# Two FFN tiles shared by chunks 1 and 2 and three shared by chunks 3 and 2, as products of 512 columns

## What is computed

```python
x = x + tanh(g_xattn) * wkv(w, u, layernorm(x), ctx)      # a decaying scan over the 128 positions
n = layernorm(x)
h = fwht(n * SU_ug) / 64                                  # Hadamard transform, 256 wide
g, up = h @ W_gate.T * (Wscale_gate * 64), h @ W_up.T * (Wscale_up * 64)   # 256 -> 1024
h = fwht(silu(g) * up * SU_dp) / 64                       # 1024 wide
x = x + tanh(g_ffn) * (h @ W_down.T * (Wscale_dp * 64))   # 1024 -> 256
```

## Time and profile before

| | us |
|---|---|
| median of 3 runs | 110.94 |
| lowest, highest | 109.91, 111.43 |
| profiled execution, its own time | 110.77 |
| its span, first to last instruction | 109.0 |
| PE busy in it | 102.0 (94%) |
| DVE, ACT, POOL busy | 69.7, 68.1, 61.2 |

### The profile page before, as it was taken

The page is one execution under the profiler, slowest core; times in us unless marked ns, Lnnn a source line. Parts: engine busy times, 40 slices in busy tenths (PEclk is TensorE's granted clock), DMA queues, the critical chain, the costliest instruction groups (busy, mean ns, idle before and its releaser), DMA issues.

```text
span 109.0 us, 2031 instructions
## 1 busy us (share of the span) xinstructions
PE 102.0 (94%) x728; PEld 92.4 (85%) x728; DVE 69.7 (64%) x146; ACT 68.1 (63%) x153; POOL 61.2 (56%) x73
## 2 busy tenths in 40 slices
PE   6999999798999999978999999699999999999990
PEld 5787797477667999968999989699999999999980
DVE  0399987599999995798998259932277221134211
ACT  4099969889929899925337995555975532442400
POOL 7026995996995994149996246355207243234400
PEclk9999999999999999999999999999999999999998
DMA  1899999200000000000000000020000200000202
GB/s 63 269 359 384 387 415 403 111 3 6 0 0 0 0 6 0 0 0 3 0 0 6 0 0 0 0 102 0 0 0 3 96 6 0 0 3 0 96 6 96
DMA packets 2893, 7.70 MB, mean 71 GB/s; under 512 B 321, under 2 KB 706, under 8 KB 2754
## 3 DMA queue, kind: packets, MB, share of 16 engines
q1 hardware_dynamic: 2882, 7.56, 18.6%
HBM read 6.51 MB, written 1.05 MB: 69 GB/s over the span
## 4 chain that ended last, share of the span: by engine, by line
PE 59%; ACT 14%; DVE 14%; issue 9%; DVEq 0%; POOL 0%; ACTq 0%; POOLq 0%
PE UG L960 24%; PE VB L833 9%; PE OD L998 5%; PE VB L998 3%; PE FX L998 3%; PE KZ L998 3%; ACT L558 2%; PE FX L923 2%; ACT L561 2%; DVE DEN L720 2%; PE FX L877 2%; DVE SQ L664 2%; PE OD L890 2%; PE VB L890 2%; PE KZ L890 2%
## 5 line engine op out<-in xcount | busy, mean ns | idle before, releaser
L478 POOL TENSOR_TENSOR HL<-H,HH 128x256 fp32r<-128x256 f32 x32 | 26.0, 817 | 30.0 <-ACT HH L617 29.9
L810 DVE SCALAR_TENSOR_TENSOR H<-S,ALPHA,UG 128x256 f32<-128x256 f32 x32 | 15.0, 476 | 17.5 <-ACT S L626 17.4
L626 ACT ACTIVATE S<-UG,HI 128x256 f32<-128x256 f32 x32 | 14.8, 467 | 14.6 <-PE UG L960 14.6
L960 PE MATMUL UG<-FH,WTH 128*128 128x256 f32 x128 | 21.8, 293 | 0.8 <-DVE H L810 0.7
L617 ACT ACTIVATE HH<-H 128x256 fp32r<-128x256 f32 x32 | 13.2, 411 | 12.3 <-DVE H L810 12.2
L960 PE MATMUL UG<-FL,WTH 128*128 128x256 f32 x128 | 20.2, 280 | 0.5 <-DVE FL L781 0.5
L960 PE MATMUL UG<-FH,WTL 128*128 128x256 f32 x128 | 20.1, 279 | 0.0
L960 PEld LDWEIGHTS UG<-FH,WTH 128*128 128x128 f32 x128 | 17.6, 189 | 2.4 <-issue 1.2
L960 PEld LDWEIGHTS UG<-FL,WTH 128*128 128x128 f32 x128 | 17.2, 189 | 0.7 <-DVE FL L781 0.7
L960 PEld LDWEIGHTS UG<-FH,WTL 128*128 128x128 f32 x128 | 17.2, 188 | 0.0
L833 PE MATMUL VB<-ONES 128*128 128x256 f32 x32 | 9.9, 470 | 1.0 <-POOL ONES L432 1.0
(11 more groups left out here) (154 smaller groups left out, 220.7 us busy)
## 6 DMA issues: line engine op xcount, KB each, us to landing
WN<-in_weights SPq DMA_DIRECT2D x4, 512.0 KB, 9.9
DN<-in_w_down SPq DMA_DIRECT2D x1, 1024.0 KB, 7.0
out<-XT SPq DMA_DIRECT2D x3, 256.0 KB, 2.5
X<-in_x SPq DMA_DIRECT2D x2, 256.0 KB, 3.9
V<-in_ct SPq DMA_DIRECT2D x2, 256.0 KB, 8.0
XT<-in_xt SPq DMA_DIRECT2D x2, 256.0 KB, 9.9
X<-in_x SPq DMA_DIRECT2D x1, 512.0 KB, 9.9
V<-in_ct SPq DMA_DIRECT2D x1, 512.0 KB, 12.7
```

The lines of the kernel that those rows point to most:

```text
L478: pool.tensor_tensor(HL[:, q % JT, 0:n], ring(H, q), HH[:, q % JT, 0:n].bitcast(F32), ALU.subtract).then_inc(h_lo, 1)
L626: act.activation(ring(S, q), gate_part(q), ACT.Silu, scale=VT[:, V_SGATE + j:V_SGATE + j + 1]).then_inc(silu_ready, 1)
L810: dve.scalar_tensor_tensor(out=ring(H, q), in0=ring(S, q), scalar=ALPHA[:, j:j + 1], in1=up_part(q), op0=ALU.mult, op1=ALU.mult).then_inc( ...
L960: return pe.matmul(dst.rearrange("p (g n) -> p g n", n=GT), w[:, m, j, t, :], f[:, chunks, t, :], start=start, stop=stop, skip_group_check ...
```

## The change

- The order of slots is now a list `PASSES`, 27 slots in place of 32: chunk 0 with tiles 0 to 7, chunk 1 with tiles 0 to 5, chunks 1 and 2 together with tiles 6 and 7, chunk 2 with tiles 0 to 2, chunks 3 and 2 together with tiles 3 to 5, chunk 3 with tiles 6, 7, 0, 1, 2. A shared slot ("wide" below: 14, 15, 19, 20, 21) has the same 12 up products and 6 down products, of 512 columns. Its gate part and its up part fill a bank each, and ACT, DVE and POOL work on 512 columns in it.
- The totals: chunk 0 has the halves of OD; then KZ holds t = 0 and OD t = 1, chunks 1 and then 3 in the left half, chunk 2 in the right half. FX and VB hold none. Between chunks 1 and 3 DVE writes zeros into the left halves (`emptied`).
- The down products follow a table `DOWNS`. None stands behind slots 13, 24, 25 and 26; the last five slots' products are left for the end (`TAIL` = 4).
- The halves of the squares aren't added by POOL any more: `ones` of chunks 2 and 3 takes two products in place of one.
- Steps move: `ones` 2 from slot 12 to 10, `fwht` 3 from 17 to 16, `ones` 3 from 19 to the same slot 16; ACT's steps with them, with `f_hi` of chunks 2 and 3 now inside the `exp_block`, ahead of the second table load.

```diff
+PASSES = (((0,), range(JT)), ((1,), range(6)), ((1, 2), (6, 7)), ((2,), range(3)), ((3, 2), range(3, 6)), ((3,), (6, 7, 0, 1, 2)))
+ROWS = [(chunks, j) for chunks, js in PASSES for j in js]
+HOME = (3, 1, 2, 0)
...
 PE_STAGES
     9: [("fwht", 2)],
-    12: [("ones", 2)],
-    17: [("fwht", 3)],
-    19: [("ones", 3)],
+    10: [("ones", 2)],
+    16: [("fwht", 3), ("ones", 3)],
 ACT_STAGES
     9: [("square", 2)],
-    12: [("exp_block", (("rstd2", 2), ("recip", 3))), ("f_hi", 2)],
-    15: [("x_hi", 3)],
-    17: [("square", 3)],
-    19: [("exp_block", (("rstd2", 3),)), ("f_hi", 3)],
+    10: [("exp_block", (("rstd2", 2), ("recip", 3), ("f_hi", 2)))],
+    14: [("x_hi", 3)],
+    16: [("square", 3), ("exp_block", (("rstd2", 3), ("f_hi", 3)))],
 DVE_STAGES
     6: [("x_lo", 2), ("scan_a", 3)],
-    8: [("mix_den", 3), ("scan_av", 3)],
-    9: [("mix_num", 3)],
-    12: [("root", 2), ("f_scaled", 2), ("f_lo", 2), ("estimate", 3)],
+    9: [("mix_den", 3)],
+    10: [("root", 2), ("f_scaled", 2), ("f_lo", 2), ("scan_av", 3)],
+    12: [("out", 0), ("mix_num", 3), ("estimate", 3)],
     13: [("newton", 3), ("x1", 3)],
-    15: [("x_lo", 3)],
-    19: [("root", 3), ("f_scaled", 3), ("f_lo", 3)],
+    14: [("x_lo", 3)],
+    16: [("root", 3), ("f_scaled", 3), ("f_lo", 3)],
+    18: [("out", 1)],
+    23: [("out", 2)],
 POOL_STAGES
-    5: [("av", 3)],
-    6: [("x1_first", 0)],
-    8: [("sum", 2)],
-    11: [("error", 3)],
-    17: [("sum", 3)],
+    6: [("av", 3)],
+    9: [("x1_first", 0), ("error", 3)],
+DOWNS = {
+    6: [0], 7: [1], 8: [2], 9: [3], 10: [4], 11: [5], 12: [6, 7], 14: [8, 9], 15: [10, 11], 16: [12], 17: [13, 14], 18: [15], 19: [16, 17],
+    20: [18], 21: [19], 22: [20], 23: [21],
+}
+TAIL = 4
...
 out_of, DVE
+                if g == 1:
+                    dve.wait_ge(out_ready, CT * g + t + 1)
+                    dve.memset(total(LAST, t), 0.0).then_inc(emptied, 1)
...
 down, PE
+                    if first(q, 0) and t == 0:
+                        wait_shared(pe, "m_lo", M_FULL[3])
+                    elif first(q, 1) and t == 0:
+                        pe.wait_ge(a_ready, NG)
+                    elif first(q, 1):
+                        pe.wait_ge(out_ready, CT)
+                    elif final(q - 1, 1):
+                        pe.wait_ge(emptied, t + 1)
...
 behind the last up, PE
+            left = range(max(r for rs in DOWNS.values() for r in rs) + 1, SLOTS)
+            for n, r in enumerate(left[:-1]):
+                pe.wait_ge(h_lo, r + 1)
...
+                down_part(r, 0)
+            for n, r in enumerate(left[:TAIL]):
...
+                down_part(r, 1)
             pe.wait_ge(h_lo, SLOTS)
             down_part(SLOTS - 1, 0)
+            for r in left[TAIL:]:
+                down_part(r, 1)
```

More of the change, by code:

```diff
@@ L33 @@
 NBANKS = 4
-LAG = 6
-TAIL = 3
 WHOLE = ()
@@ L111, in places, with first, final @@
     return [g for n, g in stages(table) if n == name]
-def group(q):
-    return q // JT
 def width(q):
-    return GT * len(GROUPS[group(q)])
+    return GT * len(ROWS[q][0])
+def first(q, g):
+    return g in ROWS[q][0] and not any(g in ROWS[r][0] for r in range(q))
+def final(q, g):
+    return g in ROWS[q][0] and not any(g in ROWS[r][0] for r in range(q + 1, SLOTS))
+UNITS = []
+for q in range(SLOTS):
+    n = width(q) // GT
+    u = UNITS[-1][-1] + 1 if UNITS else 0
+    u += u % n
+    UNITS.append(range(u, u + n))
 FILLS = []
@@ L138 @@
 M_FULL = places(PE_STAGES, "m")
+SUMMED = places(POOL_STAGES, "sum")
 SHARED = ("norm1", "av", "error", "w_lo", "m_lo", "fly", "x_lo")
@@ L235, in build @@
         e_ready, f_scaled, f_hi, f_lo = (sem(n) for n in ("e_ready", "f_scaled", "f_hi", "f_lo"))
-        silu_ready, h_ready, h_hi, h_lo, down_full, out_ready = (sem(n) for n in (
-            "silu_ready", "h_ready", "h_hi", "h_lo", "down_full", "out_ready"))
+        silu_ready, h_ready, h_hi, h_lo, down_full, out_ready, emptied = (sem(n) for n in (
+            "silu_ready", "h_ready", "h_hi", "h_lo", "down_full", "out_ready", "emptied"))
         def arrival(g):
@@ L256, in ring @@
         def ring(tile, q):
-            n, places = width(q), RING * GT // width(q)
-            return tile[:, q % places * n:(q % places + 1) * n]
+            u = UNITS[q][0] % RING
+            return tile[:, u * GT:u * GT + width(q)]
         def before(q):
-            return q - RING
+            return max([r for r in range(q) for u in UNITS[r] if u + RING in UNITS[q]], default=-1)
         def gate_part(q):
@@ L610, in stage @@
                         act.wait_ge(f_scaled, CT * g + t + 1)
-                        act.activation(FH[:, g, t, :], FN[:, t, :], ACT.Copy).then_inc(f_hi, 1)
+                        act.activation(FH[:, HOME[g], t, :], FN[:, t, :], ACT.Copy).then_inc(f_hi, 1)
             def hi(q):
@@ L815, in _ @@
                     hidden(q)
-                if q >= JT + LAG and (q - LAG) % JT == 0:
-                    for t in range(CT):
-                        out_of((q - LAG) // JT - 1, t)
                 for name, g in DVE_STAGES.get(q, []):
-                    stage(name, g)
+                    if name == "out":
+                        for t in range(CT):
+                            out_of(g, t)
+                    else:
+                        stage(name, g)
             for t in range(CT):
@@ L928, in stage @@
                     if g == 1:
-                        pe.wait_ge(squared, CT + 1)
                         wait_shared(pe, "m_lo", M_FULL[2])
+                    elif g:
+                        pe.wait_ge(e_ready, 3 * g)
+                    if g and g not in SUMMED:
+                        pe.wait_ge(squared, CT + g)
                         for t in range(CT):
@@ L944, in up @@
             def up(q):
-                g, j = divmod(q, JT)
+                chunks, j = ROWS[q]
                 n = width(q)
[L948 to L953, removed]
+                new = max([g for g in chunks if first(q, g)], default=None)
+                wait_bank_free(pe, ("up" if n == GT else "gate", q))
+                fresh = q < JT and j % 2 == 0
                 if fresh:
@@ L964, in up @@
                     for t in range(CT):
-                        if j == 0:
-                            pe.wait_ge(f_hi, CT * GROUPS[g][-1] + t + 1)
+                        if new is not None:
+                            pe.wait_ge(f_hi, CT * new + t + 1)
                         for m in range(2):
@@ L973, in up @@
                             product(m, WTL, FH, t, False, False)
-                    if j == 0:
-                        pe.wait_ge(f_lo, GROUPS[g][-1] + 1)
+                    if new is not None:
+                        pe.wait_ge(f_lo, new + 1)
                     for m in range(2):
@@ L983, in up @@
                             wait_bank_free(pe, ("up", q))
-                        if j == 0 and m == 0:
-                            pe.wait_ge(f_hi, CT * (GROUPS[g][-1] + 1))
+                        elif new is not None:
+                            pe.wait_ge(f_hi, CT * (new + 1))
                         for w, f in ((WTH, FH), (WTL, FH), (WTH, FL)):
-                            if j == 0 and m == 0 and f is FL:
-                                pe.wait_ge(f_lo, GROUPS[g][-1] + 1)
+                            if m == 0 and f is FL and new is not None:
+                                pe.wait_ge(f_lo, new + 1)
                             for t in range(CT):
@@ L993, in down_part @@
             def down_part(q, t):
-                g, j = divmod(q, JT)
-                n = width(q)
+                chunks, j = ROWS[q]
+                begins = first(q, 0) and t == 0 or first(q, 1)
+                ends = [g for g in chunks if final(q, g)]
                 for k, (m, h) in enumerate(((MH, HH), (ML, HH), (MH, HL))):
-                    a = pe.matmul(total(g, t), m[:, j, t * P:(t + 1) * P], h[:, j, 0:n],
-                                  start=(j == 0 and k == 0 and (t == 0 or g == LAST)), stop=(j == JT - 1 and k == 2), skip_group_check=True)
-                if j == JT - 1 and (t == CT - 1 or g == LAST):
+                    a = pe.matmul(totals(q, t), m[:, j, t * P:(t + 1) * P], h[:, q % JT, 0:width(q)],
+                                  start=(begins and k == 0), stop=(bool(ends) and k == 2), skip_group_check=True)
+                if ends and (t == CT - 1 or LAST in ends):
                     a.then_inc(down_full, 1)
             def down(q):
-                g, j = divmod(q, JT)
+                j = ROWS[q][1]
                 pe.wait_ge(h_lo, q + 1)
@@ L1009, in down @@
                 for t in range(CT):
[L1010 to L1023, removed]
+                    if first(q, 0) and t == 0:
[6 more added lines that the diff above has]
+                        pe.wait_ge(emptied, t + 1)
+                    elif final(q - 1, 2):
+                        pe.wait_ge(out_ready, CT * 2 + t + 1)
                     down_part(q, t)
```

56 lines of the change are left out of this document (27 added, 29 removed).

## The result

The changed kernel takes 111.33 us (median of 20 runs, 110.95 to 111.79), the kernel before 110.99 in the same comparison (109.56 to 111.43). The ratio is 1.0077 (95% interval 1.0053 to 1.0102), where I had forecast 0.2 us less. So the change costs 0.3 us by the medians of all runs, 0.5 by their means (111.36 and 110.82) and 0.85 by the ratio: small, but slower in each account. The time lies in my range, and within 2% as forecast, but the direction is wrong.

A forecast was written before the change was run, and what follows sets the result against it. PE was taken as the bound, busy 94% of the span. Waits gone -2.04, wide products -1.6, `ones` +0.86, new waits +0.95, +0.85 and +0.8, end +0.2, spacing -0.2 gave -0.2 us: 110.6 us, range 109.0 to 112.6.

The forecast's parts named there:

- the wide products: Five shared slots: 90 products of 512 columns each replace two of 256, saving 0.018 us per pair, -1.6 us.
- Rival (b): Wide products take what two narrow ones take, so PE's list isn't shortened: +1.6, 112.2 us; chance 0.11.
- Waits gone: PE's four waits between 50 and 72 us, at `fwht` 2, slot 16 and `fwht` 3, disappear: -2.04 us.
- `ones` 2: PE waits ahead of chunk 2's sum of squares for `square` 2 on ACT: +0.95 us (0.5 to 1.8).
- The longer `exp_block`: On ACT, `f_hi` 2 ahead of the silu table load delays `hidden(11)`; covered by 0.4 us, no PE wait.
- rival (a): DVE becomes the bound between 56 and 68 us, if `hidden(11)` comes after 62.8: 112.3 us; chance 0.22.
- `ones` 3: `fwht` 3 and `ones` 3 share a slot with nothing between them on PE: uncovered wait, +0.85 us.
- The end's wait: Behind the last `up`, PE waits for slot 25's `h_lo` with only three t = 0 parts as cover: +0.8 us.
- End: Behind the last products: DVE's two final operations follow at once, +0.1, and stores closer together, +0.1; +0.2 us.
- `ones` with two products: Sums of squares of chunks 2 and 3 take one more product each on PE, 2 x 0.43: +0.86 us.
- Spacing: Narrow products' start-to-start time, 0.113 or 0.118 us: taken as -0.2 us, between +0.35 and -0.7.
- The starting point: The profiled execution of the kernel before took 110.77 us, the median 0.17 above it; forecast 110.6 us.

The follow-up runs named there:

- the second comparison: The unaltered changed kernel measured once more against the kernel before: 111.43 us (6 runs), ratio 1.0103.
- the last experiment: Kernel before, narrow slots, with `av` 3 and chunk 3's `fwht` and `ones` one slot later and `x1_first` at slot 9: 108.67 us, ratio 0.9772.
- two reorderings of a few lines: Changed kernel with its last down products reordered, then also `fwht` 3 ahead of `down(12)`: 110.29 us, then 109.63 us, ratio 0.9961 to the kernel before.

## Why the prediction was wrong

The step that failed is **the wide products**: -1.6 us, from 0.018 saved per pair. I read 0.42 ns per column from the plain fp32 rows and took it for fp32r. A product of 512 takes 0.233, so a pair saves 0.003 against the slow spacing (-0.2 us over 90) and loses 0.006 against the fast one (+0.6, outside the bounds that I gave, 0 to -1.9). With -0.2 in the place of -1.6 the sum of the prediction reads +1.2 us, so this term alone turns its sign. The row that had it right was the other bound, line 906 with 0.23, the only fp32r product of that length; I set it aside for its surroundings. There was luck in that row: it counts from end to end, and from start to start that product has 0.32 us to the next (14.77 and 15.09 in the kernel before). Rival (b) is what happened; its time, 112.2, is too long, mostly as `ones` 2 waited less than I had it.

The other terms:
- **Waits gone**, -2.04: all four went. The relief of `x_lo` by POOL's `av` was right in its mechanism (0.69 us); the scan was relieved too, which I had not expected: I looked for `av` beside it, and it began before POOL did.
- **`ones` 2**, +0.95: 0.33. Less the offset of 0.56, PE came at 53.35, as in the walk (53.4), but `square` 2 ended at 53.55 and not at 54.2; most of it is the scan's 0.53 us.
- **The longer `exp_block`**: covered. `hidden(11)` ended at 62.1 and PE wanted the bank at 62.72, so the cover was 0.6 us where I had 0.4, and rival (a) did not happen.
- **`ones` 3**, +0.85: 0.94. **The end's wait**, +0.8: 0.88. **End**, +0.2: 0.25 in both profiles of the changed kernel.
- **`ones` with two products**, +0.86: as written.
- **Restarts**, at nothing in the sum: a wait costs 0.07 to 0.11 us beyond its gap, as the product behind it stands further from the next. In the sum this cancels nearly, as four waits went and three came.
- **Spacing**, -0.2: in the two profiles -0.7 (the +0.03 of the middle, less -2.04, -0.22, +0.86 and the new waits of 2.15), since the one of before had 118 ns from 71 us on and the one of the changed kernel 113 there, but for three us. I took one execution's spacing as that of the kernel. Its two profiles have both, and this term isn't a gain of the change.
- **The starting point**: the prediction names the median, 0.17 above the profiled execution, and then doesn't add it. From 110.94 its sum gives 110.8 and not 110.6.

With the measured sizes, without spacing: -2.04 - 0.2 + 0.86 + 0.33 + 0.94 + 0.88 + 0.25 = +1.0 us. Measured were +0.3 by the medians and +0.85 by the ratio of 1.0077, and in the second comparison +1.4 and +1.1 (1.0103). The measured differences lie 1.1 us apart among themselves, so they bear out the sum in its sign and rough size only; how much of that is the spacing of the kernel before stays open. The change gave up about 2.2 us in new waits and 0.86 in extra sums, and won 2.0 by moved steps that need no shared slot: the last experiment wins them on the kernel before.

## What to carry to other kernels

Price an instruction of a new size from a row of its own number format, and if there is only one such row, let it be the value and not a bound. When a rewritten schedule does two things at once, list its new waits by name and size: two reorderings of a few lines took out 1.8 us here, and left a kernel 0.4% under the one before. And take a row that repeats (a slot) from several executions before it stands for the kernel: here it had two values 4% apart.

## What the runs showed of the hardware

- An fp32r product takes 0.11 us for 128 columns, 0.113 or 0.118 for 256, 0.173 for 384 and 0.233 for 512, at a granted clock of 1.00. Plain fp32 takes 0.429 us for half a product of 512, 0.419 ns per column and pass. The rule of the Trainium skill, "TensorE: Matmul & The Clock Gate", section "Wait — 56ns, not 53.3ns?", 215.7 ns for 512 columns, fits a pass of the plain format (429 for two) and not fp32r.
- The spacing of 256-column fp32r products has two levels, 113 and 118 ns, within one execution and between executions of one kernel, at the same granted clock. It changes mostly where the row is broken, by a wait, by `ones` or by `fwht`. What picks the level stays open: no run here isolates it.
- The warming products fall from 0.427 to 0.216 us, a factor of two, at 4.4 us in one profile of the changed kernel and at 7.4 in the other (5.0 and 5.8 in the kernel before), while the granted clock shows 1.00 in all that time. The front then differs by up to 0.7 us, since PE waits for DVE where it is early.
- DVE operations with two SBUF inputs beside POOL: the same `x_lo` took 1.72 us and 0.69, the scan 1.75 and 1.22, `mix_den` (two operations) 1.37 to 2.59. Of `x_lo`, the scan and POOL's two operations beside them, the one that began second was the one that was stretched.
- Behind a wait the first fp32r product of 256 columns stands up to 0.22 us from the next, and not 0.11.
